# A graph layer with scatters through HBM: the pair summed on chip moved from groups 4 and 5 to 8 and 9, rounds dealt by an account, 20 transposes in front of the last phase

## What is computed

```
h    = relu(layernorm(x))
e    = relu(concat(h[dst], edge_attr) @ W1a.T + b1a) @ W1b.T + b1b     # one row per edge
agg  = segment_sum(e, src) / max(count(src), 1)
z    = relu(concat(h, agg) @ W2a.T + b2a) @ W2b.T + b2b
out  = x + concat(z, h) @ Wr.T + br
```

## Time and profile before

| | |
|---|---|
| median of 3 runs | 587.67 us (586.36 to 588.06) |
| the profiled execution | 587.94 us, its span 586.2 us |
| busy share of the span | TensorE 78%, GpSimd 68%, VectorE 67%, ScalarE 18% |
| mean granted clock of TensorE | 0.874 of full |
| moved to and from HBM | 66.78 MB read, 45.96 MB written |

### The profile page before, as it was taken

One profiled execution on the slowest core, in us unless ns is written; L12 is line 12 of the kernel. 1 busy time (PEld: TensorE's weight loads), 2 busy tenths in 40 slices (PEclk: granted clock), 3 DMA queues, 4 the chain that ended last, 5 costly groups with the idle time before them and its releaser, 6 DMA issues.

```text
span 586.2 us, 9900 instructions
## 1 busy us (share of the span) xinstructions
PE 458.5 (78%) x3348; PEld 421.2 (72%) x3348; DVE 393.6 (67%) x1623; ACT 108.1 (18%) x171; POOL 397.2 (68%) x427
## 2 busy tenths in 40 slices
PE   6555999999898758889878876758988588986492
PEld 5444898865788758789778766758977578875481
DVE  7549566664888637779856774557887378887481
ACT  3323311211121111212112211111211111100171
POOL 3776577767577777777777777777777777777100
PEclk9666979979899797898989977969998789999597
DMA  8983635454254494998644544979996499676321
GB/s 198 364 238 108 188 111 154 115 154 152 79 133 128 121 343 128 352 287 281 179 147 131 142 125 135 285 227 283 333 326 177 136 342 333 203 218 188 106 56 39
DMA packets 57586, 113.47 MB, mean 194 GB/s; under 512 B 9738, under 2 KB 34143, under 8 KB 57531
## 3 DMA queue, kind: packets, MB, share of 16 engines
q1 hardware_dynamic: 44731, 83.27, 47.3%
q0 software_dynamic: 12800, 29.52, 16.0%
HBM read 66.78 MB, written 45.96 MB: 192 GB/s over the span
## 4 chain that ended last, share of the span: by engine, by line
POOL 37%; PE 27%; issue 16%; DMA 7%; DVE 6%; SPq 4%; ACT 2%; POOLq 0%; DVEq 0%
POOL slots_dram L430 37%; PE bank L977 8%; PE bank L1002 8%; DMA slots_dram<-pay,pos_i 4%; PE bank L995 2%; DMA dstb<-in_dst 2%; PE bank L941 2%; PE bank L1009 2%; PE bank L1006 1%; PE bank L924 1%; DVE eo L543 1%; ACT pay L806 1%; PE bank L1066 1%; PE bank L1056 1%; SPq L331 1%
## 5 line engine op out<-in xcount | busy, mean ns | idle before, releaser
L430 POOL DMA_INDIRECT slots_dram<-pay,pos_i x400 | 393.0, 982 | 146.8 <-issue 116.4
L977 PE MATMUL bank<-pw,eo 128*128 128x128 f32 x832 | 132.2, 326 | 67.5 <-DVE eo L543 62.7
L977 PEld LDWEIGHTS bank<-pw,eo 128*128 128x128 f32 x832 | 124.3, 237 | 76.6 <-issue 72.1
L995 PE MATMUL bank<-rows,oh 128*125 128x130 f32 x1000 | 124.7, 283 | 19.0 <-DVE oh L560 19.0
L995 PEld LDWEIGHTS bank<-rows,oh 128*125 128x125 f32 x1000 | 119.0, 194 | 23.3 <-issue 21.0
L806 ACT ACTIVATE pay<-bank 128x1024 f32<-128x1024 f32 x49 | 50.2, 1024 | 387.0 <-PE bank L977 385.9
L560 DVE TENSOR_SCALAR oh<-marks,rows 128x125 f32<-128x125 f32 x500 | 104.0, 294 | 13.8 <-DMA rows<-slots_dram 13.4
L1002 PE MATMUL bank<-dense,oh 128*125 128x130 f32 x800 | 94.4, 275 | 7.8 <-issue 7.8
L1002 PEld LDWEIGHTS bank<-dense,oh 128*125 128x125 f32 x800 | 91.0, 187 | 9.8 <-issue 9.6
L555 DVE TENSOR_SCALAR oh<-firsts,dense_at 128x125 f32<-128x125 f32 x400 | 81.1, 293 | 0.4
L543 DVE TENSOR_SCALAR eo<-dstb,lane 64x256 f32<-64x256 int32 x208 | 64.0, 367 | 11.0 <-DMA dstb<-in_dst 10.2
(11 more groups left out here) (146 smaller groups left out, 269.9 us busy)
## 6 DMA issues: line engine op xcount, KB each, us to landing
rows<-slots_dram SPq DMA_DIRECT2D x32, 864.0 KB, 10.0
dstb<-in_dst SPq DMA_DIRECT2D x52, 256.0 KB, 6.2
eo<-in_edges_T SPq DMA_DIRECT2D x52, 256.0 KB, 3.8
slots_dram<-pay,pos_i POOLq DMA_INDIRECT x400
slots_dram<-zeros SPq DMA_DIRECT2D x6, 864.0 KB, 7.9
rows<-slots_dram SPq DMA_DIRECT2D x10, 432.0 KB, 3.8
rows<-slots_dram SPq DMA_DIRECT2D x16, 216.0 KB, 2.9
slots_dram<-zeros SPq DMA_DIRECT2D x3, 756.0 KB, 5.9
```

What stands on the lines that cost most here:

```text
L430: pool.indirect_dma_start(out=slots_dram[:, :], out_offset=bass.IndirectOffsetOnAxis(ap=pos_i[:, u, k:k + 1], axis=0), in_=pay[:, u, k, :] ...
L977: last = T.matmul(bank[:, 2 * (g % 2) + k // 4, (k % 4) * HID:(k % 4 + 1) * HID], eo[:, u, k * 128:(k + 1) * 128], pw[:, g % WB, a, :], st ...
L995: last = T.matmul(o[0:BN, v * SW:(v + 1) * SW], oh2[:, r % 2, n, :], rows[:, sum_no[r] % RR, n, 0:SW], start=(t == 0), stop=(t == C[ph] - ...
```

## The change

Three edits.

1. `DENSE_PAIRS` is [4] in place of [2]: groups 8 and 9 are kept on chip, groups 4 and 5 are scattered. Every phase keeps its number of pairs; phase 0 now holds the pairs 0 to 3 and 5 to 8, the first group of each phase after it stays (18, 34, 44, 48, 50).
2. The dealing of rounds. The room is now an account: each group adds 10 (23 from group 10 on), what isn't used is kept up to 32, and a round is put after a group when its whole cost is there. An h, z or check round costs 5, a dense round 16, a sum round its matmuls. A dense round may come from the group after the dense pair on, and more than one in a group. This gives: h rounds after groups 7 to 11, z rounds after 12 to 16, one dense round after each of groups 10 to 17, 19, 20, 30, 31, 33, 34 and 36, two after 18, 21, 29, 32 and 35. The sum rounds stay within one round of where they were (phase 0 after 22 to 28, phase 1 after 38 to 44, phase 2 after 46 to 49, phase 3 after 50 and 51), and the same eleven are left over.
3. TensorE, after the left-over rounds, waits for the ReLU of the last group and then transposes the identity 20 times into a PSUM bank that the tail overwrites later.

```diff
--- before.py
+++ after.py
@@ -35,7 +35,7 @@
     EPS = 1e-5
 
     PAIRS = [8, 8, 5, 2, 1, 1]
-    DENSE_PAIRS = [2]
+    DENSE_PAIRS = [4]
     DENSE_GROUPS = [2 * i + v for i in DENSE_PAIRS for v in (0, 1)]
     DK = 2 * K
     SCATTER_PAIRS = [i for i in range(NP) if i not in DENSE_PAIRS]
@@ -65,6 +65,7 @@
     EB, DB, WB, PB = 3, 4, 2, 4
 
     TPR = 12
+    BUSY = 20
     RR = 4
     Z_BUCKETS, H_BUCKETS = 4, 4
 
@@ -82,26 +83,29 @@
 
     def matmuls(v):
         kind, ph, b0, m = v
-        return m * C[ph] if kind == "sum" else DK if kind == "dense" else 2 * m
-
-    ROUNDS_FROM, A_GROUP, LEFT = 7, 28, {"sum": 10, "dense": 16, "h": 4, "z": 4, "check": 0}
+        return m * C[ph] if kind == "sum" else DK if kind == "dense" else 5
+
+    ROUNDS_FROM, FULL_FROM, EARLY_SHARE, SHARE, MOST = 7, 10, 10, 23, 32
     AFTER_PHASE = [4, 4, 2, 1, 0]
     FIRST_BAD = 2 + 2 * NPH
     rounds = []
     after = [[] for _ in range(NG)]
     queues = [[v for v in sum_rounds if v[1] < NPH - 1], dense_rounds, node_rounds]
+
+    def ready(v, g):
+        kind, ph = v[:2]
+        if kind == "sum":
+            return g >= FIRST_GROUP[ph + 1] + AFTER_PHASE[ph]
+        return kind != "dense" or g >= DENSE_GROUPS[2 * ph + 1] + 1
+
+    room = 0
     for g in range(ROUNDS_FROM, NG):
-        room = A_GROUP
+        room = min(MOST, room + (SHARE if g >= FULL_FROM else EARLY_SHARE))
         for queue in queues:
-            while queue and room >= LEFT[queue[0][0]]:
-                kind, ph = queue[0][:2]
-                if kind == "sum" and g < FIRST_GROUP[ph + 1] + AFTER_PHASE[ph]:
-                    break
+            while queue and ready(queue[0], g) and room >= matmuls(queue[0]):
                 room -= matmuls(queue[0])
                 after[g].append(len(rounds))
                 rounds.append(queue.pop(0))
-                if kind == "dense":
-                    break
     assert not queues[1] and not queues[2]
     left_over = list(range(len(rounds), len(rounds) + len(queues[0])))
     rounds += queues[0] + tail_rounds
@@ -1044,6 +1048,9 @@
                         sum_round(r)
             for r in left_over:
                 sum_round(r)
+            pe.wait_ge(S["rl"], NG)
+            for v in range(BUSY):
+                T.transpose(bank[:, 0, 0:128], ident[:], I[:])
 
             def transposes(q):
                 r, b0, m = tails[q]
```

## The result

The changed kernel takes 572.62 us (median of 4 runs, 571.86 to 572.98) against 587.01 us before in the same comparison: ratio 0.975, 95% interval 0.973 to 0.977. It is 14.4 us faster; 574.4 was forecast, with 571.2 to 579.5. In later comparisons, where the executions of a kernel fell into a faster and a slower set, a ratio is of the faster sets alone, a median of all.

A forecast was written before the change was run, and what follows sets the result against it. GpSimd's scatters set the pace from 154 us on, with 16.5 us of waits and a 42 us tail. Gains of 4.5+0.96+3.04+1.10+3.66=13.3 us, transposes 0, bring 587.94 to 574.6, median 574.4; range 571.2 to 579.5.

The forecast's parts named there:

- What bounds: Whole kernel: from 154 us on GpSimd's scatters set the pace, 1.286 us each; before, GpSimd waits, 16.5 us in all.
- Edit 1, group 4: GpSimd's first scatter of group 4: 3.2 us of waiting replace 7.74 at group 6, gain 4.5 us, bounds 2.5 to 6.4.
- Edit 2: Dealing of rounds: waits at groups 10, 12, 13 and 14 go, gains 0.96, 3.04, 1.10 and 3.66 us.
- Rival C: Groups 14 and 16: GpSimd waits again because TensorE and VectorE get no lead; 576.5 to 579.5 us, chance 0.18.
- Groups 18 to 51 at no cost: Later groups: rounds dealt anew stay hidden; a pair with three dense rounds costs 17.2 us, under 20.6 of scatters.
- VectorE at L528: VectorE's wait for the group four before to land, 58.3 us in the profile before, was to get longer.
- Edit 3: Before the tail: 20 transposes fit in a 6.93 us gap at no cost; gain 0, at most 2.2 us.
- rival B: Tail: the transposes raise TensorE's clock and it holds; 572.2 us, chance 0.20.
- The rival in e2, e5, e6 and e10: In these runs' own forecasts: transposes don't count for TensorE's clock; no chance given.
- The sum: In front of the last scatter 13.3 us are gained, so it starts near 530.8; median time 574.4 us.
- D: GpSimd: each scatter lengthens under denser traffic; at 33 ns the gain is gone, at 39 ns 590 us; chance 0.06.
- E: Group 4 is ready no sooner than group 6 was, waits of groups 10 to 14 return elsewhere; 586 to 589, chance 0.04.

The follow-up runs named there:

- second and third comparison: Later measurement calls in which every kernel, the one before included, took some 750 to 760 us; changed kernel unchanged: 758.77 and 745.73 us, ratio 1.000 in both.
- e4: Changed kernel with the dense pair back at groups 4 and 5 and no transposes, only the account left; 576.68 us, ratio 0.980 to the kernel before.
- e3: Kernel before with only the dense pair moved to groups 8 and 9, old dealing rule, no transposes; 581.10 us, ratio 0.987.
- e1: Changed kernel without the 20 transposes and their wait; 574.53 us, ratio 0.975 to the kernel before.
- e2: Kernel before with only the 20 transposes added; 588.01 us, ratio 1.000 to the kernel before.
- e5: Changed kernel with 36 transposes in front of the tail in place of 20; 764.39 us, no ratio; repeated, 749.63 us, ratio 1.010.
- e6: Changed kernel with 30 more transposes after the hidden product of group 3, before group 4; 758.90 us, ratio 1.006.
- e10: Changed kernel with 60 transposes and 30 products, results unread, behind the last store; 765.06 us, no ratio.

## Why the prediction was right, and where it was off

**What bounds.** GpSimd's cadence from 154 us on, waits before: right. The table above shows it over six kernels, as long as TensorE keeps ahead; in the second and third comparison it did not.

**Edit 1, group 4.** Forecast: 3.2 us of waiting in place of 7.74. Measured: 2.0. The reason given was right to the digit, as TensorE's timeline has it:

```profile
51.89 3.75 PE L981 MATMUL bank<-pw,eo 128*128 128x128 f32 x16 [2.49 <-DVE eo L547]
```

2.49 us of idleness for the positions, then 3.75 us at a granted clock of 0.50. The 1.2 us are the front of the kernel, which came 1.8 us earlier in this execution (the numbers of group 3 landed earlier: VectorE waited 8.6 us for them instead of 10.2), while GpSimd's own end of group 3 came only 0.5 earlier. Two independent fronts, each moving a little, carry this term by 1 to 2 us; that it came out better than forecast was luck.

**Edit 2.** Forecast: all 8.8 us of waits at groups 10 to 14 go; group 12 ready at 107 to 114; a pair then costs 25.1 us, so that group 16 has 2 us to spare. Measured: none of these waits; group 12's ReLU done at 111.3; but a pair cost 21.5 and 22.9 us (ReLUs at 110.28, 131.76 and 154.61), and group 16 had 4.5 us. The pair's price was mis-sized by 2 to 4 us: it was taken whole from groups 12 and 13 of before, which have the same dense rounds but one z round more (1.94 us), and with them the hidden product of group 14, which took 3.54 us there after 2.75 us of idleness and 2.02 us here after 0.85. The credit was rightly given to the account: alone (e4) it takes all 8.8 us, the pair alone (e3) 1.0. Rival C, the thin spare, was a sound worry all the same: 3.5 us was the smallest lead, and e3 shows how a few node rounds too many bring such a wait at once.

**Groups 18 to 51 at no cost.** Right: leads of 3.9 to 16 us, no wait. VectorE at L528 (L524 before) was forecast to wait longer; over the whole span it waited 39.1 us, where before it was 58.3 in the stretch from 195 to 545 us alone. That sign was wrong. The shorter wait goes with the account: it is 40.6 us in e4 (account alone), but 64.2 in e3 (pair alone) and 58.9 over the whole span before. Nothing hung on it, since GpSimd did not wait for VectorE there.

```profile
DVE pay L528 <- DMA slots_dram<-pay,pos_i: 39.1, 11, 10.6
```

**Edit 3.** Forecast 0, with up to 2.2 us if the clock holds (rival B). In the profile it was 1.4 us. Two grounds for the 0 failed. One was an estimate of the author: at least 2 us of idleness behind the transposes (6.93 less 4.7) would end their effect. The idleness was 3.65 us, but the granted clock stayed at 1.00 over it and fell to 0.50 only in the tail. The other is the nearest row, transposes and window projections from 22.76 on at 0.50: in the changed kernel's profile TensorE does the same work from 22.58 on, and the granted clock is at 1.00 by 26.5. But the runs do not show a gain by the transposes in the medians (e1 against the change, e2 against before), and tails of 40.9 and 41.2 us occur without them. So no run shows the 0 by itself; it was about right for the metric, by luck as far as its reasons go, and neither rival B nor its denial is settled; at most 2 us are at stake. The rival in e2, e5, e6 and e10, that transposes don't count for the clock, is contradicted by e10 for these float32 transposes: the granted clock went from 0.50 to 1.00 with nothing else running.

**The sum.** 13.3 us were forecast in front of the last scatter and 14.7 measured: the four waits at groups 10 to 14 as forecast, group 4 better by 1.2, the first scatter by 0.4. The tail gave 1.4 more in the profiled execution. By the medians the change is worth 14.4, and the time is 1.8 us under the forecast.

**Rivals D and E.** A mean scatter took 983 ns against 982: it did not lengthen. E is excluded by the interval of the first comparison.

## What to carry to other kernels

Where one engine sets the pace, sum the waits of its work items, item by item: if the cadence of the items stays (here 1.286 us), a change of order can win that sum and little more. Fill the stage in which the pacing engine starves with its own work (here: let it scatter groups 4 and 5), and deal side work by what is spent, not by a fixed count per step, so that none of it stands in front of an item that is nearly late. Ask which engine sets the pace on the day: in two comparisons in which TensorE was slower, for a reason not found, the same change showed no gain.

## What the runs showed of the hardware

Transposes alone took TensorE's granted clock from 0.50 to 1.00 of full, some 5 us after the first of them (e10). The length of an idle stretch did not tell whether the clock falls: it stayed full over 3.65 us in the changed kernel, fell about 3.1 us into the 4.73 us behind the transposes of e2, and about 1.1 us after the last product of the tail in e10. In two comparisons TensorE was idle without any releaser before many matmuls (0.8 us in the mean and at most 2.4 within rounds in one trace), and it was busy longer (539.5 and 520.6 us against 445.1 for the changed kernel) at a lower granted clock (0.792 and 0.810 against 0.908). The kernel before took 27 to 28% longer there, the changed one 30 to 33%. GpSimd's scatters, at 975 ns against 983, were not slower. What slowed TensorE was not tried.
